# Opposite alternation of two PSUM banks for the side pieces in the second pass of every attention head

## The reference

```python
x = x + attn(layernorm(x))          # 32 heads of 128, 8 key/value heads, plus a "latent" attention
x = x + ffn(layernorm(x))           # a 512x512 layer with routed low-rank additions

q, k = rope(x @ w_q), rope(x @ w_k)          # 32 query heads, 8 key heads (4 query heads share one)
v = x @ w_v
lq = x @ w_lq                                # 128 wide
lk, lv = rope(lq @ w_lk), x @ w_lv           # 32 latent key and value heads
attn = softmax(causal(q @ k.T / sqrt(128))) @ v
lat  = softmax(causal(q @ lk.T / sqrt(128))) @ lv
return attn @ w_o + lat @ w_lo
```

## Time and profile before

| | |
|---|---|
| three runs, us | 2163.46, 2163.77, 2166.22; median 2163.77 |
| profiled execution, its own time | 2163.13 us |
| its span, first to last instruction | 2161.4 us (1.7 us lie around it) |
| PE busy | 2079.6 us, 96% |
| PE weight loads busy | 1757.8 us, 81% |
| DVE, ACT, POOL busy | 73%, 53%, 41% |
| granted TensorE clock | 0.998 of 2.4 GHz |

### The profile page before, as it was taken

The page is one execution under the profiler, slowest core; times in us unless marked ns, Lnnn a source line. Parts: engine busy times, 40 slices in busy tenths (PEclk is TensorE's granted clock), DMA queues, the critical chain, the costliest instruction groups (busy, mean ns, idle before and its releaser), DMA issues.

```text
span 2161.4 us, 32460 instructions
## 1 busy us (share of the span) xinstructions
PE 2079.6 (96%) x11236; PEld 1757.8 (81%) x11236; DVE 1577.7 (73%) x2946; ACT 1140.6 (53%) x2502; POOL 884.0 (41%) x693
## 2 busy tenths in 40 slices
PE   5999999999999999999999999999999999999988
PEld 4888888888788888888888888888878888888877
DVE  6777777777777777777777777777777777777775
ACT  2555545555455555555455554555545555555541
POOL 4433443434533344443533344343453334444311
PEclk9999999999999999999999999999999999999999
DMA  2111111111011111111111111111211112111121
GB/s 95 36 35 37 38 30 41 41 36 45 26 41 27 40 46 30 41 32 41 36 36 35 37 38 30 41 41 37 45 26 41 27 41 46 30 41 32 41 50 39
DMA packets 101840, 83.71 MB, mean 39 GB/s; under 512 B 28200, under 2 KB 73896, under 8 KB 101680
## 3 DMA queue, kind: packets, MB, share of 16 engines
q1 hardware_dynamic: 101680, 81.65, 15.2%
HBM read 79.26 MB, written 2.36 MB: 38 GB/s over the span
## 4 chain that ended last, share of the span: by engine, by line
PE 76%; DVE 16%; issue 4%; ACT 3%; POOL 1%; DMA 0%; DVEq 0%; SPq 0%; ACTq 0%
PE scores L414 9%; PE scores L416 9%; PE scores L415 9%; PE bankX L414 8%; PE bankT L476 8%; PE bankX L416 8%; PE bankX L415 8%; PE bankO L414 5%; PE bankO L416 5%; PE bankO L415 5%; DVE rot_half L977 4%; DVE rot_half L976 3%; DVE probs L960 3%; DVE o_raw L1031 2%; DVE PT_lo L966 1%
## 5 line engine op out<-in xcount | busy, mean ns | idle before, releaser
L701 ACT ACTIVATE PT_hi<-bankT 128x512 fp32r<-128x512 f32 (+2 forms) x640 | 337.1, 533 | 406.4 <-PE bankO L416 341.8
L966 DVE TENSOR_TENSOR PT_lo<-bankT,PT_hi 128x512 fp32r<-128x512 f32 (+2 forms) x640 | 387.4, 609 | 197.8 <-ACT PT_hi L701 192.7
L760 ACT ACTIVATE probs<-probs,nmax 128x128 f32<-128x128 f32 (+7 forms) x512 | 394.8, 773 | 138.0 <-DVE nmax L960 137.9
L960 DVE CUSTOM_DVE_ANT_0 probs<-scores,mask 128x128 f32<-128x128 f32 (+7 forms) x512 | 381.3, 749 | 66.8 <-PE scores L416 65.6
L476 PE MATMUL bankT<-ident,probs 128*128 128x128 f32 x2304 | 379.1, 273 | 7.6 <-DVE PT_lo L966 2.0
L476 PEld LDWEIGHTS bankT<-ident,probs 128*128 128x128 f32 x2304 | 285.2, 140 | 75.6 <-DVE PT_lo L966 20.7
L1193 POOL TENSOR_TENSOR rot<-rot,cos 128x512 f32<-128x512 f32 x144 | 185.7, 1289 | 218.0 <-DVE rot_half L977 218.0
L1187 POOL TENSOR_TENSOR OT_lo<-o_raw,OT_hi 128x512 fp32r<-128x512 f32 x64 | 83.0, 1296 | 409.8 <-ACT OT_hi L701 409.8
L1195 POOL TENSOR_TENSOR rot<-rot,rot_half 128x512 f32<-128x512 f32 x144 | 207.2, 1439 | 11.3
L701 ACT ACTIVATE OT_hi<-o_raw 128x512 fp32r<-128x512 f32 x128 | 80.9, 632 | 193.7 <-DVE o_raw L1031 152.6
L976 DVE TENSOR_TENSOR rot_half<-rot,sin 64x512 f32<-64x512 f32 x144 | 108.2, 751 | 85.6 <-ACT rot L701 82.1
(11 more groups left out here) (241 smaller groups left out, 5197.7 us busy)
## 6 DMA issues: line engine op xcount, KB each, us to landing
inv_b<-inverses SPq DMA_DIRECT2D x128, 256.0 KB, 4.0
stage<-in_L_attn_w_q SPq DMA_DIRECT2D x32, 256.0 KB, 4.9
stage<-in_L_attn_w_lv SPq DMA_DIRECT2D x32, 256.0 KB, 2.8
stage<-in_L_attn_w_o SPq DMA_DIRECT2D x32, 256.0 KB, 5.0
stage<-in_L_attn_w_lo SPq DMA_DIRECT2D x32, 256.0 KB, 2.6
acc<-in_L_attn_hidden_states SPq DMA_DIRECT2D x2, 1024.0 KB, 6.9
stage<-in_L_attn_w_k SPq DMA_DIRECT2D x8, 256.0 KB, 5.0
stage<-in_L_attn_w_v SPq DMA_DIRECT2D x8, 256.0 KB, 5.3
```

The source lines that it names most:

```text
L701: return act.activation(place, src, ACT.Copy)
L760: act.activation(prob_tile(c, t), prob_tile(c, t), ACT.Exp, bias=nmax[:, c, t:t + 1], scale=-1.0, accum_out=rsum[:, c, t:t + 1]).then_inc( ...
L960: dve.tensor_tensor_reduce(place, src, tile_view(mask[:, S - width:S], c), -SCALE, -MASKED, ALU.add, ALU.min, nmax[:, c, t:t + 1]).then_in ...
L966: dve.tensor_tensor(pt_place(1, hh, w, j), bankT[j % 2][:, block_columns(c, j):CH], f32(pt_place(0, hh, w, j)), ALU.subtract).then_inc(pt_ ...
```

## The change

One line. In pass 1 the alternation begins with bank 1 in place of bank 0; passes 0, 2 and 3 are as they were.

```diff
         def piece_bank(hh, w, s, more):
 
-            return sorted(pieces_of(w, hh, more)).index(s) % 2 if w in (1, 3) else 0
+            return (sorted(pieces_of(w, hh, more)).index(s) + (w == 1)) % 2 if w in (1, 3) else 0
```

## The result

The changed kernel took 2144.5 us (median of 4 runs, 2143.8 to 2150.1) beside 2165.0 us for the kernel before (4 runs, 2163.5 to 2167.5): ratio 0.9906, 95% interval 0.9889 to 0.9923. The profiled execution took 2144.28 us, its span is 2142.5. Against the span before, 2161.4, that is 18.9 us.

A forecast was written before the change was run, and what follows sets the result against it. PE's own stream, busy 96% of the span, was taken as the bound. Removing 30.7 us of LV1 waits and putting back 10.2 gave net 20.5 us off 2163.13: 2142.6 us, range 2138 to 2156 for 8 in 10.

The forecast's parts named there:

- The bound and the place of the wait: PE's stream bounds; LV1 waits for LV0's copy in bank 0; vT waits fall from 39 to 7.
- The price of a wait from start to start: At LV1: 0.86 us late plus 0.10 for the unhidden load, 0.96 per head, 30.7 us in all.
- The costs set to nothing: First and last OUT1 tiles and the other five pieces of pass 1 change banks at cost 0.
- The narrow case: In a group's last head, scaled `o_raw` ahead of pass 1's first product keeps 0.17 us: cost 0, narrowly.
- What is late next: First latent score tile of pass 1 waits for POOL's `LKT_lo`, which doesn't move; eats 0.32 us per head.
- Whether the load is hidden: Score tile's weight load waits with its matmul, gain 0.64 us per head; were it hidden, 0.74.
- That the gain lasts: DVE's idle 0.41 and 1.07 us in pass 1 absorb the 0.64 shift; each head is 0.64 shorter.
- part was given back: Rival: later in the head, transposes' 0.30 us margin leaves only 0.24 us per head, 2155.4 us; chance 0.13.
- The end of the sum: Over 32 heads: 30.7 us removed, 10.2 put back, net 20.5 us, giving 2142.6 us.
- a granted clock below 0.998: In the changed kernel's profile: named as a sign that the prediction was wrong.
- the full gain: Rival: 2132.4 us, needing `LKT_lo` 0.40 us or more earlier; chance 0.06.
- The slower one: Rival: `out_low` ahead of `LKT_lo`, which ends 1.28 us later; loss 0.64 per head, about 2184 us; chance 0.05.

The follow-up runs named there:

- POOL's order: Changed kernel, with POOL making the low half of LK0 ahead of LK1's rotary sum: ratio 0.9862 to the kernel before, 2133.6 us.
- first four pieces: Kernel before, with only the pieces at steps 0 to 3 of pass 1 taking the opposite banks: ratio 0.9910.
- pass 3 flipped: Kernel before, with the opposite alternation in pass 3 in place of pass 1, in the first three heads of every group: ratio 0.9998.
- two experiments: Changed kernel with one POOL subtraction more ahead of `LKT_lo`: 1.0191; kernel before with DVE copying LV0 ahead of LK1's rotary product: 1.0112.
- kernel with waits of 1.75 us per head: Changed kernel with one POOL subtraction more, into a spare tile, ahead of `LKT_lo`: ratio 1.0191 to the kernel before, 2207.8 us.

## Why the prediction was right

The median is 2144.5 us, predicted were 2142.6 with a range of 2138 to 2156.

*The bound and the place of the wait:* right. 32 waits went and 7 stayed, as worked out from the two counts.

*The price of a wait from start to start, 0.96 us:* the total is right, 1.63 - 0.67 = 0.96; its two parts are not, and that they add up is luck. The prediction had LV1 start 0.86 late and lose 0.10 more by a weight load that wasn't hidden. Now that nothing waits, LV1 starts 955.31 - 954.96 = 0.35 behind the transposes, not 0.44, so it was 0.95 late. Its second matmul follows after 0.32 even so, against 0.33 behind the wait, and its load begins 0.03 ahead of it. The step of 0.24 that the prediction compared with belongs to the middle of the stream. Both mistakes, 0.09 each, cancel. The idle time in brackets, 0.69, would have made it 22 us in all. The sum of bank change and POOL's order, 0.94 per head, shows the full price in the measured time.

*The costs set to nothing:* right. The later pieces of pass 1 (first four pieces) and banks as such (pass 3 flipped) have no effect that these runs can tell. The first OUT1 tile starts at 959.99, long after the copy that it waits for (956.19). The narrow case held too: PE waits for the scaled output 8 times, 3.4 us in all, in both kernels.

*What is late next:* right in place and engine: 32 waits for POOL's `LKT_lo`. The size was a little off: 0.35 to 0.36 us put back per head, 0.32 predicted. The load began 0.05 behind POOL's end (959.48 to 959.53) and the second matmul 0.23 behind it, against 0.045 and 0.22 in the sum. The rest is POOL: in a typical head `LKT_lo` ends 15.35 us after LK0's start, where it was 15.33, so it did move by 0.02 to 0.03. 32 x 0.605 = 19.4 us against 20.5. The predicted waits of the loads, 0.4 us each, were 0.52: that view counts from the end of the load before, which is earlier than the point where the next one was due. At the matmul itself the view shows little, as predicted: the idle time ahead of the matmuls of this kind (L414 `scores<-LKT_hi,QT_lo`) went from 5.0 to 7.5 us, 0.08 per head.

*Whether the load is hidden:* the load waited with its matmul, both at 959.53, and the second matmul came 0.11 us later behind the first than undisturbed (0.23 in place of 0.12). The Trainium skill's rule ("TensorE: Matmul & The Clock Gate", Part 2) of loads pulled ahead does not hold across a semaphore wait in these runs. Where nothing waits, the rows agree with it: the same load stood 0.23 us ahead of its matmul before (969.78 and 970.01).

*That the gain lasts:* right. Heads gain one by one, and DVE's idle times of 0.41 and 0.22 us took up the shift; the one of 1.07, on which the prediction leaned as well, was not needed. No part was given back in pass 1.

*The end of the sum:* 18.9 us of span against 20.5. Of the 1.6 missing, 1.1 is the new wait's size and 0.5 lies outside the heads, in start-up and tail, which the sum didn't have. The prediction had named a granted clock below 0.998 as a sign of being wrong, and it is 0.997. That comes from the tail alone: over the 31 heads it is 1.00 in both kernels.

*The rivals:* the full gain was refused by `LKT_lo`, and came as soon as that was made earlier. The slower one, the exchange of order between `out_low` and `LKT_lo`, did not occur in the changed kernel: POOL still starts 958.60 - 958.17 = 0.43 us ahead. But it is real, two experiments ran into it. The prediction's 1.28 us was made of 0.43 for POOL's slip and 0.85 for the whole of `out_low`. In the two experiments POOL was issued with 0.6 us of `out_low` left, and its subtraction was 0.43 longer; the full 0.85 occurred in no run. The Trainium skill ("SBUF — State Buffer", Who interferes with whom) has such a lock, by which the second to issue is blocked until the first is done. These rows agree with its order: of a DVE instruction with two inputs in SBUF and a POOL instruction beside it, the one issued second is the longer. They show less than a full block: 0.43 longer with 0.6 left, and 0.58 longer for `out_low` (1.42 against 0.84) with 0.86 of POOL's subtraction left.

## What to carry to other kernels

When two jobs share a buffer across the seam of two stages, look which pair stands closest there: an alternation that is right inside each stage can put the same buffer on both sides of the seam, and turning its phase cost nothing here. Price a wait of TensorE from matmul start to matmul start, up to the second matmul behind the wait, and take the undisturbed distance from the same kind of seam, not from the middle of a stream. Then move everything behind it forward by that price and look for the first release that doesn't move; the gain is capped there, and an edit that makes that release earlier may be worth nothing alone and, as here, over a third of what both bring together (10.4 of 29.2 us).

## What the runs showed of the hardware that I had not expected

- In the kernel with waits of 1.75 us per head TensorE lost its full clock in 6 of 31 heads (1.6 us each), 0.8 to 1.5 us after such a wait. In the other kernels, with waits of up to 1.5 us there, it did not in any head behind the first. A stall can so cost twice.
- DVE and POOL stretch each other by which of them was issued first. `out_low` on DVE takes 0.84 us when it starts ahead of POOL's subtraction, and 1.43 when it starts 0.4 us behind; POOL's subtraction takes 1.72 in the first case, and 1.29 in the second. An instruction of DVE that was moved to save 0.96 us of PE's time per head cost 1.1% in this way and by its idle time.
- In the tail the two profiled executions spent different stretches at 1.2 GHz, with the same wait of 3.5 us ahead of them, and in the same 20 us near the start one had full clock (1.00) and the other 0.91. Over the eleven profiled executions the start differs by 6 us and the tail by 3. A few us of difference at either end therefore mean nothing; the time between two like matmuls in the first and last head does.
